# The last attention head also prepares the feed-forward: attention and feed-forward in one code block

## The reference

```
q, k, v = x @ w_aq, x @ w_ak, x @ w_av          # 8 heads of 128
q, k = rope(q), rope(k)
p = softmax(q @ k.T / 128, causal)              # per head, 1024 x 1024
x = layernorm(x + sum over heads of (p @ v) @ w_ao)
h = silu((x @ w1.T) * s1) * ((x @ w2.T) * s2)    # 128 -> 512
h = gelu((h @ h1.T) * t1)                        # 512 -> 512
h = gelu((h @ h2.T) * t2)                        # 512 -> 512
x = layernorm(x + (h @ w3.T) * s3)               # 512 -> 128
```

## Time and profile before

| | |
|---|---|
| median of three runs | 1062.29 us |
| the profiled execution | 1063.32 us |
| its span, first to last instruction | 1061.5 us |
| PE busy (matmuls) | 995.9 us, 94% |
| DVE busy | 828.7 us, 78% |
| ACT busy | 593.5 us, 56% |
| POOL busy | 539.5 us, 51% |
| mean granted clock of TensorE | 0.978 |

### The profile page before, as it was taken

One profiled execution on the slowest core, in us unless ns is written; L12 is line 12 of the kernel. 1 busy time (PEld: TensorE's weight loads), 2 busy tenths in 40 slices (PEclk: granted clock), 3 DMA queues, 4 the chain that ended last, 5 costly groups with the idle time before them and its releaser, 6 DMA issues. The chain is left out here.

```text
span 1061.5 us, 19675 instructions
## 1 busy us (share of the span) xinstructions
PE 995.9 (94%) x5648; PEld 859.2 (81%) x5648; DVE 828.7 (78%) x1803; ACT 593.5 (56%) x1255; POOL 539.5 (51%) x536
## 2 busy tenths in 40 slices
PE   3799999999999999999999999999839999999995
PEld 2688898888888888898988889888728878788784
DVE  5888888888888888888888888888465677586744
ACT  3566666665666666666766666666334252433521
POOL 4666767776677776767676676776150101000000
PEclk8899999999999999999999999999869999999998
DMA  8533233332232223232222322221020000000000
GB/s 282 168 110 78 63 79 104 114 96 70 65 79 60 49 60 102 68 75 65 59 49 60 81 66 75 50 59 41 1 79 1 1 1 21 1 20 0 1 20 21
DMA packets 33291, 66.16 MB, mean 62 GB/s; under 512 B 5456, under 2 KB 6992, under 8 KB 32208
## 3 DMA queue, kind: packets, MB, share of 16 engines
q1 hardware_dynamic: 30400, 58.62, 21.0%
q10 hardware_dynamic: 2832, 6.82, 1.8%
HBM read 24.26 MB, written 7.34 MB: 30 GB/s over the span
## 5 line engine op out<-in xcount | busy, mean ns | idle before, releaser
L703 POOL TENSOR_SCALAR probs<-probs,inv_sum 128x128 f32<-128x128 f32 (+7 forms) x256 | 191.3, 747 | 226.8 <-DVE inv_sum L621 226.4
L534 ACT ACTIVATE pT<-psum 128x512 fp32r<-128x512 f32 (+3 forms) x384 | 174.0, 490 | 133.4 <-PE psum L401 131.4
L308 PE MATMUL psum<-pT,vals 128*128 128x512 f32 (+3 forms) x1152 | 243.9, 352 | 2.3 <-DVE rT L663 2.3
L522 ACT ACTIVATE probs<-psum,neg_max 128x128 f32<-128x128 f32 (+7 forms) x256 | 190.2, 743 | 84.9 <-DVE neg_max L615 82.7
L631 DVE TENSOR_TENSOR pT<-psum,pT 128x512 fp32r<-128x512 f32 (+3 forms) x384 | 200.9, 551 | 30.8 <-ACT pT L534 26.8
L615 DVE TENSOR_REDUCE neg_max<-psum 128x1 f32<-128x128 f32 (+7 forms) x256 | 191.5, 748 | 28.1 <-PE psum L392 27.0
L308 PEld LDWEIGHTS psum<-pT,vals 128*128 128x128 f32 x1152 | 189.6, 191 | 25.3 <-DVE pT L631 2.5
L883 PE MATMUL ps<-hid,w 128*128 128x512 f32 x768 | 181.4, 396 | 0.0
L401 PE MATMUL psum<-ident,probs 128*128 128x128 f32 x1152 | 172.4, 276 | 8.2 <-POOL probs L703 5.9
L883 PEld LDWEIGHTS ps<-hid,w 128*128 128x128 f32 x768 | 143.8, 188 | 34.4
L708 POOL TENSOR_TENSOR swapped<-by_cos,swapped 128x512 f32<-128x512 f32 x128 | 164.5, 1296 | 14.1 <-DMA swapped<-by_sin 14.1
(11 more groups left out here) (77 smaller groups left out, 1137.5 us busy)
## 6 DMA issues: line engine op xcount, KB each, us to landing
swapped<-by_sin SPq DMA_DIRECT2D x256, 128.0 KB, 2.3
w_stage<-qk_split SPq DMA_DIRECT2D x30, 256.0 KB, 2.6
wv_stage<-v_split SPq DMA_DIRECT2D x15, 256.0 KB, 2.7
x_split<-ffn_raw ACTq DMA_DIRECT2D x2, 1024.0 KB, 5.3
ffn_raw<-g SPq DMA_DIRECT2D x2, 1024.0 KB, 8.2
x_moving<-x_split SPq DMA_DIRECT2D x2, 1024.0 KB, 5.1
out<-y SPq DMA_DIRECT2D x4, 512.0 KB, 2.6
raw_x<-xT SPq DMA_DIRECT2D x3, 512.0 KB, 11.8
```

Of the source, the lines that this page charges most:

```text
L308: ins = nc.tensor.matmul(out_ap, left[a], right[b], start=first and i == 0, stop=last and i == 2)
L522: nc.scalar.activation(probs[:, ib % 4, :width].rearrange("p (h c) -> p h c", h=halves), score_ps[:, ib % 2, :halves, :half], ACT.Exp, bia ...
L534: nc.scalar.activation(pT[chunk][:, 0, 4 * f:4 * f + n_blocks, (ib % 4) * P:(ib % 4 + 1) * P], bank("t", head[1], nth)[:, :n_blocks * P].r ...
L703: nc.gpsimd.tensor_scalar(p, p, inv_sum[:, n:n + 1], 1.0, ALU.mult, ALU.mult).then_inc(probs_ready[0], 1)
```

## The change

Attention and feed-forward become one code block, so no engine waits for all others between them. The feed-forward is now a class `FeedForward`, whose pieces are called from attention's steps of the last head ("s" is the step):

| engine | what is added to the last head |
|---|---|
| SP | behind its last work for attention it waits for the last scores of head 30, then issues the three loads of tokens and scales |
| PE | s 0: transposes of the first 1024 tokens' result, into banks 4 and 1; s 7, behind the transposes of block 7: transposes of the normalised `y` |
| DVE | s 1: the two additions to `y`; s 2: statistics; s 3: means, variance, seed; s 4: first round of the root; s 5: the other two, and the shift; s 6: the eight normalising instructions; s 7: the addition of chunk 0, moved here from the drain, ahead of the subtraction of block 7; drain, s 0: the low part of the turned `y` |
| ACT | s 1 to 7: a high piece of the weights (512 columns each) at the end of each step; s 7: one Silu of 128x1, ahead of the copies of block 7 (it loads Silu's table) |
| POOL | s 2 to 7: a low piece of the weights (512 columns) behind the step's other work |

Behind the last step: ACT splits the turned `y` and the four high pieces that are left, POOL the five low ones. The gated layer's first group waits for both halves of the split `y` and two weight pieces, its second also for the last addition of attention. The tensors are laid out anew: the split weights lie over attention's staging tensors (so ACT in s 1 and DVE in s 6 wait until these are no longer read), `y` over q and k of the even heads. The passes themselves are as before.

```diff
@@ wait_for_banks
+                if (b in USES[ORDER[at]] and kind == "qk" and nth < CHUNKS and isinstance(back, int)
+                        and number((back, off)) == HEADS):
+                    ffn.wait_for_first_r(pe, nth)
+                    break
@@ sync
+            wait_for(sp, scores_ready, (PAIRS - 1, 0), NI - 1)
+            ffn.load_tokens(sp)
+            ffn.sync_program(sp)
@@ tensor
+                if is_last(head) and s == 0:
+                    for c in range(CHUNKS):
+                        wait_for_banks(pe, head[0], "qk", 2, c)
+                        ffn.turn_first_r(pe, c, bank("qk", 2, c))
+                if is_last(head) and s == NI - 1:
+                    for c in range(CHUNKS):
+                        wait_for(pe, exp_done, head, 6 + c)
+                        ffn.turn_first_y(pe, c)
@@ scalar
+                if is_last(head) and s == NI - 1:
+                    ffn.load_silu(act)
                 if exists(head):
                     transposed_high(head, s)
                 for c in v_tasks(head, s):
                     values_high(head[0], c)
+                if is_last(head) and s >= 1:
+                    if s == 1:
+                        wait_for_stages(act)
+                    ffn.weights_high(act, s - 1)
@@ vector
-                if s == ADD0_STEP:
+                if s == ADD0_STEP and not is_last(step_on(head, -1)):
                     add_head(step_on(head, -1), 0)
+                if is_last(head) and s == NI - 1:
+                    add_head(head, 0)
                 if exists(head):
                     transposed_low(head, s)
+                if is_last(head):
+                    if s == 1:
+                        for c in range(CHUNKS):
+                            ffn.add_first_r(dve, c, bank("qk", 2, c))
+                    if s == 2:
+                        ffn.norm_stats(dve, 0, 0)
+                    if s == 3:
+                        ffn.norm_means(dve, 0, 0)
+                    if s == 4:
+                        ffn.norm_root(dve, 0, 0, 0)
+                    if s == 5:
+                        ffn.norm_root(dve, 0, 0, 1)
+                        ffn.norm_root(dve, 0, 0, 2)
+                        ffn.norm_shift(dve, 0, 0)
+                    if s == 6:
+                        wait_for_stages(dve)
+                        ffn.normalize_first(dve)
+                if is_last(step_on(head, -1)) and s == 0:
+                    ffn.first_low(dve)
@@ gpsimd
+                if is_last(head) and s >= 2:
+                    ffn.weights_low(pool, s - 2)
@@ FeedForward.gated_layer
+                    if first and (o, c) == (0, 0):
+                        wait_two(pe, self.yT_low, two, 1)
+                    if first and (o, c) == (0, 1):
+                        pe.wait_ge(*self.all_added)
@@ FeedForward
+    def weights_high(self, act, i):
+        if i == 0:
+            act.wait_ge(self.ffn_loaded, 80)
+        piece = slice(i * BANK, (i + 1) * BANK)
+        self.nc.scalar.activation(self.w[:, 0, piece], self.raw[:, piece], ACT.Copy).then_inc(self.w_high, 1)
```

More of the change, by code:

```diff
@@ L110, in build, with run @@
         ffn_loaded = sem("ffn_loaded")
[L111 to L119, removed]
+        run(nc, ctx, sem, rT, ident, x_split, qk_split, v_split, xT, w_q, w_k, w_vT, w_o, rope, ident_in, mask_in,
+            ffn_raw, (f1, f2, g1, g2, f3), ffn_loaded, x_tok, scales, out)
+def run(nc, outer, sem, rT, ident, x_split, qk_split, v_split, xT, w_q, w_k, w_vT, w_o, rope_in, ident_in, mask_in,
+        ffn_raw, ffn_weights, ffn_loaded, x_tok, scales_in, out):
+    ctx = outer.enter_context(ExitStack())
     def sb(name, shape, dt=F32, where=ctx):
         return where.enter_context(nc.sbuf_tensor(name, shape, dt))
+    ident_r = sb("ident_r", [P, P], F32R, outer)
+    mask_r = sb("mask_r", [P, P], F32R, outer)
+    ffn = FeedForward(nc, outer, sem, rT, ident, ffn_raw, ffn_loaded, x_tok, scales_in, out)
     rope = sb("rope", [P, 2, T])
-    ident_r = sb("ident_r", [P, P], F32R)
-    mask_r = sb("mask_r", [P, P], F32R)
     w_stage = sb("w_stage", [P, 2, 4, P], F32R)
@@ L129, in attention @@
     x_moving = sb("x_moving", [P, 2, 2, T], F32R)
-    qk = sb("qk", [P, 2, 2, 2, T], F32R)
     by_sin = sb("by_sin", [P, 2, BANK])
@@ L133, in attention @@
     swapped = sb("swapped", [P, NQK, BANK])
+    qk = sb("qk", [P, 2, 2, 2, T], F32R)
     pre = ExitStack()
@@ L152, in attention @@
     inv_sum = sb("inv_sum", [P, 2 * NI])
-    psum = ctx.enter_context(nc.psum_tensor("psum", [P, 8 * BANK], F32))
+    ctx.close()
+    ffn.place_tensors()
+    psum = outer.enter_context(nc.psum_tensor("psum", [P, 8 * BANK], F32))
     score_ps = psum[:, :4 * BANK].rearrange("p (s h c) -> p s h c", s=2, h=2)
@@ L195, in attention @@
     pool_passed = sem("pool_passed")
+    ffn.use_psum(psum, (pv_added[0], HEADS * CHUNKS))
     def score_halves(ib):
@@ L269, in v_tasks, with is_last, wait_for_stages @@
         return [c for c in range(NV) if V_STEP[c] == NI * head[1] + s and exists(head)]
+    def is_last(head):
+        return isinstance(head[0], int) and number(head) == HEADS - 1
+    def wait_for_stages(eng):
+        last = (PAIRS - 1, 1)
+        wait_for(eng, cos_done, last, NQK - 1)
+        wait_for(eng, rope_low, last, NQK - 1)
+        wait_for_pair(eng, v_projected, PAIRS - 1, NV - 1)
     def is_first(head):
@@ L477, in _ @@
             run_pairs(pe, step)
+            ffn.tensor_program(pe)
         @block.scalar
@@ L581, in step @@
                     values_high(head[0], c)
+                if is_last(head) and s >= 1:
+                    if s == 1:
+                        wait_for_stages(act)
+                    ffn.weights_high(act, s - 1)
             run_pairs(act, step)
+            ffn.scalar_program(act)
         @block.vector
@@ L690, in _ @@
             run_pairs(dve, step)
+            ffn.vector_program(dve)
         @block.gpsimd
@@ new lines, in _, with known, wait_two @@
+            ffn.gpsimd_program(pool)
+TWO = TOKENS // (2 * BANK)
+PER = BANK // P
+F1, F2, G1, G2, F3 = FFN_AT
+S1, S2, SG1, SG2, S3 = 0, HT, 2 * HT, 3 * HT, 4 * HT
+RSQRT_STEPS = 3
+RSQRT_SEED = float(0x5F3759DF)
+LINKS = 6 + 3 * RSQRT_STEPS
+TERMS = ((0, 0), (0, 1), (1, 0))
+PIECES = FFN_COLS // BANK
+PIECES_OF = {base: end // BANK for base, end in ((F1, G1), (G1, G2), (G2, F3), (F3, FFN_COLS))}
+def known(two):
+    return not isinstance(two, int) or 0 <= two < TWO
+def wait_two(eng, signal, two, nth):
+    if known(two):
+        eng.wait_ge(signal[0], signal[1] * two + nth + 1)
```

724 lines of the change are left out of this document (382 added, 342 removed).

## The result

The changed kernel takes 1039.11 us (median of 4 runs, 1038.31 to 1039.48) against 1062.19 for the kernel before, a ratio of 0.9781 (95% interval 0.9767 to 0.9795). Its profiled execution has a span of 1037.7 us, against 1061.5: 23.8 less.

A forecast was written before the change was run, and what follows sets the result against it. TensorE was taken to bound the kernel throughout except at the attention/feed-forward seam. Gap removed -20.85, later second product +5.3 and clock -2.2 gave -17.7 us: 1044.6 us from the median, range 1041 to 1050.

The forecast's parts named there:

- whatever moves its start moves the end alike: Feed-forward: once the gated layer starts, TensorE sets the pace to the end, so a shifted start shifts the end equally.
- the last of the signs of being wrong: Feed-forward after its first layer: running at another pace than before would show the prediction wrong.
- Gap removed: Seam between the last head's second product and the gated layer: TensorE's gap disappears, 20.85 us saved.
- PV1 later by 5.3: Last head's second product (24 matmuls): starts 5.3 us later because VectorE's added work bounds the head; bounds 3.6 to 9.3.
- The meetings with GpSimd: Last head, steps 3 to 5: VectorE's small instructions wait for GpSimd's weight pieces; 0.4 us taken, ceiling about 3.
- Rival C: Last head: VectorE can't use its old idle time, second product 9.3 us late, not 5.3; 1048.6 us, chance 0.11.
- Step 1: Last head: block 4's scores wait for VectorE's additions of r, starting at 746.2, 1.7 late; maximum at 747.4.
- rival B: Last head: normalising and small VectorE instructions each let a whole GpSimd piece pass; 3 us, 1047.6 us, chance 0.20.
- PV1's length: Last head's second product: 7.66 us before and after, half clock at first; about 4.9 with the clock up.
- Rival A: Last head's second product: clock doesn't fall or is back at its start; 2.8 us shorter, 1041.8 us, chance 0.14.
- The clock under the gated layer: First gated layer: 48 matmuls at full clock take 11.30 us instead of 13.49, 2.2 us saved.
- Rivals D and E: D: half clock persists into feed-forward, 1067.2 us, chance 0.02. E: late inputs move the gap into head 31, chance 0.03.

The follow-up runs named there:

- f3: Kernel before, old seam, padded so that w, y, yT and hid all start at multiples of 512 bytes: 1055.52 us, ratio 0.9934.
- e3: Changed kernel with GpSimd waiting for the normalised y before its weight piece in step 6 and those behind it: 1034.13 us, ratio 0.9738.
- f4: Changed kernel with the edits of e3 and e4, and the last two root rounds and the shift moved from step 5 to step 6: 1035.46 us, ratio 0.9742.
- e1: Kernel before with 32 unused bytes ahead of y, so feed-forward tensors behind the scales start at multiples of 64 bytes: ratio to before 0.9997.
- f1: Kernel before with 288 unused bytes ahead of y, so y, yT and hid start at multiples of 512 bytes, w unmoved: 1061.98 us, one run.
- f2: Kernel before with w moved to a multiple of 512 bytes, and y, yT and hid 256 past one: 1055.44 us, one run.
- g1: Kernel before with 160 unused bytes ahead of y, so w, yT and hid all stand 128 past a multiple of 256 bytes: 1055.85 us, one run.
- g2: Kernel before with w at a multiple of 512 bytes, but yT and hid 128 past a multiple of 256: 1060.65 us, one run.
- g3: Kernel before with yT and hid 192 past a multiple of 256 bytes, w at 128 as before: 1057.21 us, one run.
- e2: Changed kernel with 32 unused bytes ahead of hid, while w, y, r_stage and yT stay in place: 1044.25 us, ratio 0.9832.
- e4: Changed kernel with the eight normalising instructions behind VectorE's last subtraction, and y turned ahead of the last product's last third: 1036.06 us, ratio 0.9758.

## Why the prediction was wrong

The direction, the mechanism of the seam and the 2 to 3 us of clock were right; the time fell out of the range, and the step that failed is one sentence, "whatever moves its start moves the end alike": the feed-forward behind the start of the gated layer was taken to run as before, a term that the sum put at zero without a bound. The change also lays the feed-forward's tensors out anew. That I had used only for hazards, not for speed, and no rival had it, though the last of the signs of being wrong, a feed-forward at another pace after its first layer, names just this, and it is what happened. It is worth 6.46 us behind the first gated layer in the profiles and 7.0 us by itself (f3). With it the forecast would have been 1044.6 - 7.0 = 1037.6. Without the 6.46 the profiles give -17.34 against the -17.7 of the sum. That this is so close is in part luck, since errors of 2.7, 1.4 and 0.6 us cancelled:

- **Gap removed**, 20.85: right. Nothing else was late, neither weight pieces nor the last addition nor the token load.
- **PV1 later by 5.3**: measured 6.65. Two parts. The normalising instructions took 5.15, not 2.43: 2.7 more. The rest came out lower, by about 1.4: at 761.62 they began 1.2 before the 762.8 of my sum (767.3 less 0.1, 1.29, 0.69 and 2.43). The meetings with GpSimd ahead of them aren't the reason: 0.09 at the variance step and 0.36 in step 5 are 0.45, against the 0.4 that I took. The maximum of block 4 came 0.24 earlier, the 0.4 of issue gaps weren't there, and attention's own instructions, now back to back, took less than the 11.45 of the earlier trace rows, for a record then mostly begins 0.05 to 0.09 us ahead of the end of the one before it. VectorE was busy 14.00 of 16.24 us in the window of the earlier trace rows: DVE-bound, as forecast. Rival C, stalls kept, is out (its 9.3 should read 9.2 by its own terms, 1.7 + 7.5; nothing hangs on it).
- **Step 1**: the scores of block 4 waited for the addition of r. Expected start 746.2, maximum 747.4; the trace has

```profile
745.89 0.38 PE L410 MATMUL psum<-qk 128*128 128x320 f32 x1 [0.82 <-DVE y L1186]
```

  and the maximum at 747.16.
- **The port (rival B, 0.20)** was the mechanism that held. I had argued against it from the earlier trace rows: 2.43 us beside one POOL copy of 0.66. Alone these eight take 2.22 (e3) or 2.13 (f4), so that row did hold a wait of 0.2 to 0.3, which I took for nothing, having no undisturbed row beside it. And one short copy isn't three pieces of 1.24 back to back, each taken between two of the eight. The account that fits is that of the Trainium skill, "SBUF — State Buffer", section "Who interferes with whom", which says that whichever of the two comes later blocks for the other's whole instruction. This trace agrees: the three instructions that met a piece took 1.30 to 1.32 us instead of 0.34, 5.15 less 2.22 is 2.9 us, against 3.72 us of pieces, and e3 removes it. B's price, 3 us, was right, though it counted two pieces at step 6 and one before, where all three were at step 6.
- **PV1's length**: taken as 7.66, measured 7.05 (768.62 to 775.67), since the clock came back after 5 us of it and not 6 (0.64 granted over 6.98 us). But to take either for a property of the kernel is a mistake of mine: when the clock falls and comes back differs between executions. With the old seam untouched PV1 took 7.66 us in the profile of the kernel before, 6.43 or 6.44 in e1, f1, f2, g1, g2 and g3, and in f3, where the granted clock stayed at 1.00 through it,

```profile
762.57 4.84 PE L308 MATMUL psum<-pT,vals 128*128 128x512 f32 x24 [2.26 <-DVE rT L663]
```

  So the 0.6 is smaller than what executions differ by, and the account from span to span holds for these two executions. Rival A, no lower clock at PV1, didn't happen in this one; f3 shows that it can, without any change to the seam, and its 4.84 is near the 4.9 that A was priced from.
- **The clock under the gated layer**, 2.2: measured 2.53, at 1.00; 0.3 of it (48 by 6.7 ns) is the placement.
- **Rivals D and E** are out: the clock is full from the gated layer on, and the loads were in time.

Put together: -20.85 + 6.65 - 0.61 - 2.53 - 6.46 = -23.8.

## What to carry to other kernels

When a change lays out memory anew, the matmuls' pace is part of what it changes: look at the time from one matmul to the next before and after, and in fp32r products of this shape keep the distance between stationary and moving operand at a multiple of 256 bytes where that costs only a pad. Here a single tensor of 68 bytes, the scales, had put everything behind it 96 bytes off. When preparation is moved beside another phase, put each instruction behind, not ahead of, the one that the critical chain needs from the same queue, and keep VectorE's SBUF-to-SBUF tensor_scalar away from runs of GpSimd's instructions. A row that shows an operation undisturbed must be compared with one in which it is alone; "hardly slower" beside one short neighbour bounds nothing.

## What the runs showed of the hardware

TensorE's pace in fp32r products of 512 columns depends on where its two SBUF operands lie relative to each other: 227.5 ns from matmul to matmul over a run of 192 (43.68 / 192) at distance 0 modulo 256 bytes, 229.7 at 64, 233.2 at 128 and 234.2 at 32 and 96. What in the memory does this isn't shown by these runs. Attention's products have nothing to gain by this measure: the sizes of its tensors put their operands a multiple of 256 bytes apart in both kernels already.

GpSimd's weight pieces (1.27 us each) beside VectorE's two-scalar tensor_scalar cost it most of their length: the eight take 5.15 us beside three pieces, 5.21 in e2 (three as well), 3.11 in e4 beside one, 2.13 to 2.22 alone. One instruction that meets a piece takes 1.30 to 1.32 us instead of 0.34.

The granted clock around a short idle stretch isn't the same in each execution: the same 24 matmuls behind the same wait of 2.26 to 2.27 us took 7.66, 6.44 and 4.84 us.
